# Inverse deviations as exp(-ln(v + eps) / 2) with one Newton step, in a two-layer attention and expert kernel

## The reference

```python
def _layernorm(x, axis=-1, eps=1e-05):
    m = jnp.mean(x, axis=axis, keepdims=True)
    v = jnp.var(x, axis=axis, keepdims=True)
    return (x - m) / jnp.sqrt(v + eps)

x = L0_attn_in_features                                   # 16 x 256 x 128
x = x + _L0_attn_ref(_layernorm(x), Wq, Wk, Wv, Wo)       # causal softmax, 16 heads
x = x + _L0_ffn_ref(_layernorm(x), ...)                   # 8 experts, top 2
x = x + _L1_attn_ref(_layernorm(x), wq, wk, wv, wo)       # linear attention, no softmax
x = x + _L1_ffn_ref(_layernorm(x), ...)                   # 8 experts, top 1
```

## Time and profile before

| | us |
|---|---|
| median of three runs | 647.6 (645.21, 647.6, 650.58) |
| profiled execution | 643.63 |
| its span, first to last instruction | 641.9 |

### The profile page before, as it was taken

How to read it: one execution, slowest core, us unless ns; L and a number is a source line. 1 busy time by engine, 2 the same in 40 slices (tenths; PEclk the granted TensorE clock), 3 DMA queues, 4 the chain that set the end, 5 groups by cost and what they waited for, 6 DMA issues and landing times.

```text
span 641.9 us, 15198 instructions
## 1 busy us (share of the span) xinstructions
PE 528.6 (82%) x4931; PEld 438.2 (68%) x4931; DVE 461.9 (72%) x1320; ACT 350.9 (55%) x894; POOL 341.8 (53%) x459
## 2 busy tenths in 40 slices
PE   3088999999999989977597989999986474849995
PEld 2046666666667666654497989999875363849995
DVE  6477777877998799755676776555897967775672
ACT  2014557555655565544374846666756573825762
POOL 2104444444377546664754777778762552554555
PEclk9659999999999999996698999999996675998998
DMA  6563444444444444417331323324853122444320
GB/s 169 107 150 78 108 109 106 104 98 105 93 110 128 116 91 112 97 39 292 82 80 50 95 81 96 89 76 122 257 204 98 50 75 84 124 146 113 97 78 20
DMA packets 59531, 69.44 MB, mean 108 GB/s; under 512 B 9241, under 2 KB 50657, under 8 KB 57148
## 3 DMA queue, kind: packets, MB, share of 16 engines
q1 hardware_dynamic: 51744, 53.01, 32.0%
q0 software_dynamic: 7168, 14.77, 6.9%
q10 hardware_dynamic: 540, 0.69, 0.6%
HBM read 45.31 MB, written 23.67 MB: 107 GB/s over the span
## 4 chain that ended last, share of the span: by engine, by line
DVE 17%; PE 17%; issue 7%; POOL 6%; DVEq 3%; ACT 1%; DMA 1%; SPq 0%; ACTq 0%; POOLq 0%
PE h_ps_e L1863 7%; PE y_ps_e L1873 6%; POOL expert_rows L1273 5%; DVEq L1420 3%; DVE wb_e L1424 3%; DVE x L1497 1%; DVE xn_e L1526 1%; PE l_ps_e L1947 1%; PE xT_ps_e L1851 1%; DVE stats L1501 1%; DVE yt_e L1430 1%; DVE stats L1535 1%; DVE rxr L1531 1%; ACT hT_e L1709 1%; PE h_ps_e L1930 1%
## 5 line engine op out<-in xcount | busy, mean ns | idle before, releaser
L616 DVE TENSOR_REDUCE mx<-max_ps 128x2 f32<-128x512 f32 (+1 forms) x192 | 128.3, 688 | 48.4 <-PE max_ps L277 46.3
L1709 ACT ACTIVATE hT_e<-h_ps_e,wb_e 128x128 f32<-128x128 f32 x448 | 122.4, 388 | 29.6 <-PE h_ps_e L1863 28.8
L457 ACT ACTIVATE pT<-sc_ps 128x1536 f32<-128x1536 f32 x64 | 92.9, 1452 | 76.0 <-PE sc_ps L305 75.6
L1424 DVE COPY wb_e<-wpack 128x1156 f32 x112 | 84.0, 792 | 51.5 <-issue 40.5
L1863 PE MATMUL h_ps_e<-xT_e,wb_e 128*128 128x128 f32 x896 | 115.8, 285 | 2.0 <-ACT hT_e L1709 1.1
L1863 PEld LDWEIGHTS h_ps_e<-xT_e,wb_e 128*128 128x128 f32 x896 | 110.5, 201 | 3.6 <-ACT xT_e L1700 1.7
L1873 PE MATMUL y_ps_e<-wb_e,hT_e 128*128 128x128 f32 x896 | 110.0, 276 | 1.8 <-DVE yt_e L1430 1.7
L1873 PEld LDWEIGHTS y_ps_e<-wb_e,hT_e 128*128 128x128 f32 x896 | 105.4, 193 | 2.2 <-DVE yt_e L1430 2.2
L1273 POOL DMA_INDIRECT expert_rows<-yt_e,go_e x72 | 79.1, 1098 | 32.4 <-issue 19.1
L862 POOL TENSOR_TENSOR turn<-eps 128x1 f32<-128x1 f32 x64 | 12.4, 194 | 141.5 <-ACT pT L457 141.4
L58 POOL DMA_INDIRECT expert_queues<-rxr,rseats x64 | 66.5, 1039 | 26.0 <-issue 17.1
(11 more groups left out here) (277 smaller groups left out, 933.6 us busy)
## 6 DMA issues: line engine op xcount, KB each, us to landing
wpack<-in_wpack SPq DMA_DIRECT2D x2, 4112.0 KB, 15.2
parts_scratch<-parts SPq DMA_DIRECT2D x16, 384.0 KB, 2.7
xt_e<-expert_queues SPq DMA_DIRECT2D x40, 129.0 KB, 2.2
xt_e<-expert_queues SPq DMA_DIRECT2D x72, 64.5 KB, 2.0
wpack<-parts_scratch SPq DMA_DIRECT2D x24, 192.0 KB
kst<-parts_scratch SPq DMA_DIRECT2D x24, 192.0 KB
qst<-parts_scratch SPq DMA_DIRECT2D x72, 64.0 KB
wpack<-parts_scratch SPq DMA_DIRECT2D x63, 64.0 KB
```

The costliest lines, as they stand in the source:

```text
L457: nc.scalar.activation(pT[u][:], sc_ps[:].rearrange("p a s -> p (a s)"), ACT.Exp, scale=float(DH) ** -0.5).then_inc(probs_ready, 1)
L616: nc.vector.reduce_max(mx[:, s, h0:h0 + n], max_ps[:, (k + 1) % 2, :].rearrange("p (h k) -> p h k", h=n), axis=AX.X).then_inc(unit_reduced, 1)
L1424: nc.vector.tensor_copy(wb[i % 4][:, s, :], wpack[:, bass.ds(es[s], 1), :].rearrange("p a f -> p (a f)")).then_inc(w_ready, 1)
L1709: last = nc.scalar.activation(hT[i % 2][:, s, c, :], h_ps[h_bank(i)][:, s, c * RT:(c + 1) * RT], ACT.Relu, bias=wb[i % 4][:, s, FF + c:FF ...
```

## The change

Every deviation is now made inverse on ScalarE, with two activations: Ln of (v + eps), then Exp with scale -0.5 into `rstd`, the second behind a wait on the first (`log_ready`). VectorE then does one Newton step (`refine_rstd`), three linked operations, instead of the one reciprocal. For closed groups one more operation gives the deviation, (v + eps) * rstd, which `join_terms` needs, and `join_terms` waits for it (`std_ready`). One table set that holds Ln and Exp, and the cheap functions, is named at the start of the program. All dummy activations but the first go. This applies at 17 places: two groups in the first prologue, three in A bodies, the last ten tiles, six closed and five routed groups.

```diff
+def refine_rstd(nc, link, t, tt):
+    ntmp, rstd = t["ntmp"], t["rstd"]
+    link(nc.vector.scalar_tensor_tensor(out=ntmp[:, 0, tt], in0=ntmp[:, 3, tt], scalar=EPS, in1=rstd[:, tt], op0=ALU.add, op1=ALU.mult))
+    link(nc.vector.scalar_tensor_tensor(out=ntmp[:, 0, tt], in0=ntmp[:, 0, tt], scalar=-0.5, in1=rstd[:, tt], op0=ALU.mult, op1=ALU.mult))
+    link(nc.vector.scalar_tensor_tensor(out=rstd[:, tt], in0=ntmp[:, 0, tt], scalar=1.5, in1=rstd[:, tt], op0=ALU.add, op1=ALU.mult))
...
             def route_deviations(g):
                 first, n = ROUTED[g]
                 act.wait_ge(r_var_ready, g + 1)
-                nc.scalar.activation(ntmp[:, 4, first:first + n], ntmp[:, 3, first:first + n], ACT.Sqrt, bias=t["eps"][:]).then_inc(r_std_ready, 1)
-                nc.scalar.activation(idle[:], t["eps"][:], ACT.Exp)
+                nc.scalar.activation(ntmp[:, 4, first:first + n], ntmp[:, 3, first:first + n], ACT.Ln, bias=t["eps"][:]).then_inc(log_ready, 1)
+                act.wait_ge(log_ready, g + 3)
+                nc.scalar.activation(rstd[:, first:first + n], ntmp[:, 4, first:first + n], ACT.Exp, scale=-0.5).then_inc(r_rstd_ready, 1)
...
             def prologue():
+                nc.scalar.preload_act_table_set("natural_log_exp_and_others")
                 act.wait_ge(eps_ready, 1)
-                nc.scalar.activation(idle[:], t["eps"][:], ACT.Sqrt)
+                nc.scalar.activation(idle[:], t["eps"][:], ACT.Ln)
...
-                dve.wait_ge(std_ready, n)
-                nc.vector.reciprocal(rstd[:, ts], ntmp[:, 4, ts]).then_inc(scaling, 1)
-                dve.wait_ge(scaling, 4 * n)
+                dve.wait_ge(rstd_ready, n)
+                refine_rstd(nc, link, t, ts)
...
             def route_inverse(g):
                 first, n = ROUTED[g]
-                dve.wait_ge(r_std_ready, g + 1)
-                link(nc.vector.reciprocal(rstd[:, first:first + n], ntmp[:, 4, first:first + n]))
+                dve.wait_ge(r_rstd_ready, g + 1)
+                refine_rstd(nc, link, t, slice(first, first + n))
...
-            def inverse(n, first, k):
-                dve.wait_ge(std_ready, n + 1)
-                link(nc.vector.reciprocal(rstd[:, first:first + k], ntmp[:, 4, first:first + k]))
+            def scaled(n, first, k, std):
+                tt = slice(first, first + k)
+                dve.wait_ge(rstd_ready, n + 1)
+                refine_rstd(nc, link, t, tt)
+                if std:
+                    nc.vector.scalar_tensor_tensor(out=ntmp[:, 4, tt], in0=ntmp[:, 3, tt], scalar=EPS, in1=rstd[:, tt],
+                                                   op0=ALU.add, op1=ALU.mult).then_inc(std_ready, 1)
...
             def join_terms(first, n):
                 tt = slice(first, first + n)
+                dve.wait_ge(std_ready, 1 + [(first + n - 1) // TPS < a + k for a, k in SCALED].index(True))
...
-            def deviations(n, first, k):
+            def inverse_deviations(n, first, k):
                 act.wait_ge(var_ready, n + 1)
-                nc.scalar.activation(ntmp[:, 4, first:first + k], ntmp[:, 3, first:first + k], ACT.Sqrt, bias=t["eps"][:]).then_inc(std_ready, 1)
+                nc.scalar.activation(ntmp[:, 4, first:first + k], ntmp[:, 3, first:first + k], ACT.Ln, bias=t["eps"][:]).then_inc(log_ready, 1)
+                act.wait_ge(log_ready, n + 2)
+                nc.scalar.activation(rstd[:, first:first + k], ntmp[:, 4, first:first + k], ACT.Exp, scale=-0.5).then_inc(rstd_ready, 1)
...
                 if i - 1 in routed:
-                    deviations(root_routed(i - 1), *LATER[routed[i - 1]])
-                    if i not in closes:
-                        prepare(ACT.Exp, 2 * routed[i - 1])
+                    inverse_deviations(root_routed(i - 1), *LATER[routed[i - 1]])
...
                 if i in closes:
                     n, k = SCALED[closes[i]]
-                    deviations(root_closed(i), TPS * n, TPS * k)
-                    if i - 1 in routed:
-                        prepare(ACT.Exp, 2 * routed[i - 1])
+                    inverse_deviations(root_closed(i), TPS * n, TPS * k)
...
                 for g in choices(i - 1):
                     weigh_choice(g)
-                    if g < len(LATER) - 1:
-                        prepare(ACT.Sqrt, 2 * g + 1)
```

## The result

The kernel after took 653.05 us (median of 20 runs, 649.27 to 657.31), the kernel before 648.64 us (20 runs beside them, 645.21 to 651.87): the ratio is 1.0062, 95% interval 1.0042 to 1.0083, so 2.7 to 5.4 us slower, 4.0 at the middle. I had forecast 653.2 us and +5.6. At some times the unchanged kernel before took 702 or 710 us instead of 648, so ratios from such times are compared only with each other.

The account below looks back on a forecast made before the run. VectorE was taken to bound the kernel at most of these places, ScalarE holding 1% of the chain. Terms of 0.5 + 1.14 + 0.40 + 1.16 + 0.67 + 0.84 + 0.29 + 0.62 = 5.6 us on 647.6 gave 653.2, range 646.5 to 657.5.

Parts of the forecast that it names:

- R4: Second block: the set is not taken as loaded, Ln and Exp each bring a load; 671.4 us, chance 0.03.
- R1: Faster: the slots' loads decide, 646.0 us; with each of 19 switches holding the path 1.28 us, 628.8; chance 0.09.
- Step 1: Prologue: xn waits for Exp and the Newton step, +0.62, of which transfers may take part back; +0.5 us (0 to 0.6).
- Step 2: Three A bodies: the loads bring nothing, VectorE's additions cost 0.38 each; +1.14 us (0.7 to 1.2).
- Step 3: Last ten tiles: the reciprocal lies in a VectorE stretch running to the seats, the loads bring nothing; +0.40 us.
- 4 slots 0 to 5: Forecast as slots 0 to 3: three closed groups, +0.46, +0.24 (Exp ahead of ScalarE's copies) and +0.46; +1.16 us.
- Step 5: Slots 5 and 6: load on the chain, its removal gains 0.17, VectorE's two inverses cost 0.38 + 0.46; +0.67 us.
- Step 6: Slots 9 and 10: two inverses on VectorE without the gap, the dummies' loads beside VectorE work; +0.84 us.
- Steps 7 and 8: Scatters from 514.25: VectorE's 1.22 mostly covered by slack, +0.29; last group: VectorE waits for Exp and step, +0.62 us.
- R2: No change: additions swallowed by VectorE's waits for TensorE and by GpSimd's mask in the A bodies; 647.6 to 649.5, chance 0.14.
- R3: Slower over 1%: GpSimd slows three or four new VectorE operations in the slots, +1.8 to +2.4 us; 655.3, chance 0.14.

Follow-up runs that it names:

- e1: Kernel before with two further linked VectorE operations ahead of each of its 17 reciprocals, Sqrt, loads and dummies kept: 652.66 us, ratio 1.0055 to before.
- e3: Kernel after with 18 table loads of the same set put back at the old places: 653.99 us, ratio 1.0067 to before.
- e4: Kernel after once more, unchanged, for a second profiled execution: 652.98 us, ratio 1.0061 to before.
- e2: Kernel after without the Newton step, the closed groups' fourth operation kept: 643.79 us, ratio 0.9892 to before.
- g1: Kernel after with GpSimd's two mask operations per unit of the first attention shrunk from 128 x 512 to 128 x 8: 650.8 us in its one run.
- f5: Kernel after without the Newton step and with 18 table loads put back, beside a before of 702 us: 701.7 us, ratio 0.9978.
- g2: Kernel after without the Newton step and with 18 loads back, repeated beside a before of 710.48 us: 706.2 us, ratio 0.9906.
- g3: Kernel after without the Newton step, repeated beside a before of 710.48 us: 707.59 us, ratio 0.9974.
- f8: Kernel before once more, unchanged, for a second profiled execution: 702.82 us, ratio 1.0033.
- g4: Kernel after with the Newton step left out in the first block only, beside a before of 710.48 us: 713.12 us, ratio 1.0063.

## Why the prediction was right, and where not

The time and the sign were right, and for the reason given: VectorE's two further operations are on the path, ScalarE's 22 us are not (e1, e3). That 653.2 lies 0.2 us from the median of 653.05 is luck in part: the starting point of 647.6 was 1.0 us under the median of the 20 runs of before, and +5.6 was 1.2 more than the 4.4 between the medians. R4 did not occur (one load). R1 with every switch on the path would have 18 loads cost 23 us; e3 shows 0.4. The Trainium skill ("ScalarE: Activation LUTs", What ACT_TABLE_LOAD costs) gives 2.66 us for a switch to a different set, by which I estimate 48 us for 18. The row of a load of before, which does switch, shows no drain around it; e3's loads bring back the set in use, and what they cost in time is not that price. The terms compare less well than the sum:

| step | forecast | traces |
|---|---|---|
| 1 prologue | 0.5 | xn +0.61; first exponential at 49.6 to 50.2 us in the four executions with Exp and step there, mean 49.9; 48.1 to 49.9 in the ten others, mean 48.8: +1.1 |
| 2 A bodies | 1.14 | 0 + 1.16 + 1.15 = 2.3 |
| 3 last ten tiles | 0.40 | last oT to slot 0: 154.92, e4 154.97: +0.1; e1 154.25, e2 153.26 |
| 4 slots 0 to 5 | 1.16 | 21.34 to 22.43 (e4): +1.1 |
| 5 slots 5 to 7 | 0.67 | -0.14 |
| 6 slots 7 to 11 | 0.84 | 17.31 to 20.19 (e4): +2.9; e1 +1.9 |
| 7, 8 scatters, last group | 0.91 | slot 11 to the end of the span: 133.40 to 133.68 (e4): +0.3; all 14 traces 133.2 to 134.5 |

- Prices: Exp and hand-over 0.24 and the step 0.38 were as costed.
- Step 1: of the first exponential's +1.1 only the 0.6 of xn is read from the rows; the rest lies within what the executions differ by.
- Step 2 failed twice. In the first A body I took VectorE to be without a gap because the timeline printed none; it had some too short to be printed, and the last rxr row took 1.04 instead of 1.14. The largest lies between the end of this row of before (118.80) and the reduction at 118.94:

```profile
117.66 1.14 DVE L689 TENSOR_SCALAR rxr<-x,mean,rstd 128x128 f32<-128x128 f32 x2
```

  The reduction behind it starts 11.91 us after the oT copy in before, 11.89 in after, and the body kept its length, as R2 had it. In the second and third I took 0.38 of delay for 0.38 of loss. The delay pushed the four operations under GpSimd's, which held them for 1.01 us more together, and this wait is nothing that the sum has: it has only the step's own length. That is R3, in a place where I hadn't looked for it: I had priced it for the slots alone. e1 and g1 show it.
- Step 5: I said the load's removal gains only 0.17 us since VectorE would be next, and charged the step in full. The load did gain 1.38 us when there was nothing else on VectorE (10.54 against 11.92); with the step in place it gains 0.18, as I had said, but the step then costs nothing against before, since load and step lie side by side (e1: 12.02, as before). What was wrong is the base. The gap of 0.17 is what VectorE has left with its work released late; the length of its chain from the variance to xn was the quantity to read beside that of the load: 3.52 us in before, 4.32 in e1, 4.33 in e4.
- Step 6 came out 2 us over the forecast: besides the step it holds a collision with GpSimd of 1.7 us where before's was 0.6. This is R3 as I had priced it (0.6 each), except that one hit is nearly three times as dear. How much of the 2.9 is the step and how much the collision is not separated: e2 has the collision and no step, and is 1.55 us longer there than before.
- Steps 7 and 8: I had said 0.91 and the traces show 0.3, less than they differ by without any step (133.4 to 134.5). That the landings of the scatters cover the rest is not shown. Step 3's 0.40 is as little to be read from its stretch.

The traced terms add up to 7.6 us, and 4.0 (2.7 to 5.4) were measured. The difference I can't place. The same is seen in e2, whose traced A bodies and slots are as before's while its runs are 5 to 9 us shorter: the trace of before is of an execution 5.0 us under the median, and what its usual execution has more than that one is in no trace of that time. That the loads account for it was not shown (e3 against after 0.4 us; e2 and f5 are of different times, and g2 and g3 overlap).

The best version is e2, 0.9892 (0.9861 to 0.9922); the same kernel as g3, beside a kernel before of 710 us, had 0.9974 (0.9927 to 1.0021), which is not told from before. It leaves the deviation as exact as Exp and Ln make it.

## What to carry to other kernels

Taking work from an engine that waits buys nothing until the next engine in line is also shorter: read, for each place, the length of both chains between the same two events, and put the longer one down. Before adding small operations to a busy VectorE, look at what GpSimd computes half a microsecond later; a delay moves the operations behind it, and may move them under GpSimd's. And check where a profiled execution lies among its own runs before subtracting two of them.

## What I had not expected of the hardware

- Table loads of 1.28 us can be nearly free 18 times over: 23.1 us of ScalarE for 0.4 us of time, with some 2 us either way (e3). Where VectorE has nothing to do beside it, one costs its full length (slots 5 to 7, 1.38 us).
- VectorE's f32 operations from and to on-chip SBUF tiles are held while GpSimd runs one: 128x128 took 0.58 to 1.22 us instead of 0.34, each ending 0.08 us behind the mask or `parts` beside it, and 128x4 took 1.86 instead of 0.17, held through three of GpSimd's four of 128x128. The reductions from PSUM beside the same masks kept their 0.68.
- The kernel before took 649 and 710 us on one and the same chip. In the seven traces of the second kind (f5 to f8, g2 to g4) the slots' operations on VectorE are as long as ever, four bodies are 3 to 12 us longer each, and the stretch from the last oT copy to slot 0 took 181.3 to 184.8 us instead of 153.3 to 155.0.
